# A three-layer graph network on one core: table scales from a bound, and the first layer's tables made while records are being scattered

## The chip, the core and the metric

The kernel runs on one core of a Trainium2 chip. The core has five engines with instruction streams of their own: TensorE (PE, matrix products; PEld is its weight load), VectorE (DVE), ScalarE (ACT), GpSimd (POOL) and SyncE (SP, which here only issues DMAs). They wait for one another on semaphores. SBUF holds the tiles, PSUM the results of PE. The metric is the device time of one execution in microseconds (us).

## The reference, cut to what matters

```python
N, E, D, EF, L = (3125, 100000, 128, 16, 3)      # nodes, edges, width, edge features, layers
s2 = jnp.concatenate([src, dst])                  # each edge in both directions
d2 = jnp.concatenate([dst, src])
ef2 = jnp.concatenate([ef, ef], axis=0)
h_prev = nf
for l in range(L):
    e_in = jnp.concatenate([h_prev[s2], h_prev[d2], ef2], axis=-1)
    msg = jax.nn.leaky_relu(e_in @ We1[l]) @ We2[l]
    red = jax.ops.segment_sum(msg, d2, num_segments=N)
    n_in = jnp.concatenate([h_prev, red], axis=-1)
    out = jax.nn.leaky_relu(n_in @ Wn1[l]) @ Wn2[l]
    h_prev = out + h_prev
x = _layernorm(x + out, axis=-1)                  # out of the last layer, before its addition to h_prev
```

## The kernel before

The nodes are padded to 3200, 25 blocks of 128, and lie transposed in SBUF (`hT`, 128 features by 3200 nodes). The part of `We1` that meets node features is applied once for each node and not for each edge. It gives two **tables** for each layer, `a = h @ We1[0:128]` and `b = h @ We1[128:256]`. Each table value is stored as a pair of 16-bit floats, a high half and a low half, scaled by a power of two so that they fit; plane 0 of a block is the high half, plane 1 the low one, and plane 2 holds plane 0 once more. Messages are then made by one-hot matrix products that pick table rows. Since `We2` is linear, it is moved behind the sum and multiplied into the node weights: `w21 = We2 @ Wn1[128:256]`.

The kernel runs through these stages on all engines:

- **Sorting**, up to 123 us: each edge gets a place in an order by pairs of node blocks. DVE is the busiest engine.
- **Scatters**, 123 to 1124 us: GpSimd issues 784 indirect DMAs (L651), each of which writes 128 edge records to `records` in DRAM. While they run, DVE and PE work out the places of the next records; they finish at 1082 us with the `map` and `word` tables (L1033 to L1035), which tell the loop which node block each tile of edges meets. At the end GpSimd waits until records have moved, reads two counts (L434, `live_counts`, in which `live_n` is the number of turns a layer needs, 26 here) and starts the next stage.
- **Preparation loop**, 1127 to 1198 us: 30 batches of records are loaded (`recc`), transposed by PE (L1283), copied by ACT and DVE to `recT` and `numT`, and written by SP to `feat_d` (two DMAs, L544) and `nums_d` (one, L547). When it ends SP appends a copy of the first pieces behind the last ones (L551, L552, "the wrap") and waits for that. Then it loads the first numbers (`load_numbers`, L556, two) and features (`load_features`, L563, six DMAs for three parts). `recT` lies in the tiles `numb` and `gsel`, which these loads and the one-hot of them (`gather_one_hot`, L1069) fill, so they could not start before the preparation loop is done.
- **Tables of the layer** (`tables(l)` on PE, L1299; L1079 to L1126 on DVE; L757 to L772 on ACT). PE makes a and b in 13 steps of two node blocks; ACT copies each from PSUM to SBUF (L757); DVE takes the largest magnitude of each copy (L1083, 13 of them) and of all (L1086); GpSimd takes it over all partitions (L675); DVE works out the scale (L1090 to L1103) and the scaled edge weights `wst` (L1107 to L1115). ACT then writes the high halves (L772, 5 parts), DVE plane 2 (L1122) and the low halves (L1123), and at last plane 2 of the lows in one copy of 3200 (L1126). In between ACT zeroes all of the PSUM sums (L760) and copies the transposed `We2` and `w21` (L765, L767).
- **Loop of the layer**: 26 turns of 12 steps, each step three tiles of 128 edges in both directions. PE starts with `start(l)` (its first product is L1342), then gathers (L1342, L1349) and sums (L1410); ACT copies and splits (L782 to L791); DVE applies leaky_relu and the low halves (L1065, L1136), in layer 0 also the one-hots (L1069, L1153). PE reads where to add from a row of words: layer 0 with L1416, layers 1 and 2 with `keep_row` (L1494), three of them ahead of the loop.
- **Node stage** (`node(l)`): ACT copies the sums out (L797), PE makes `z` (L1424, L1425), ACT copies it to `zbuf` (L802), DVE applies leaky_relu (L1065), PE makes `out` (L1430), DVE adds it to `hT` (L1182), ACT copies it to `outT` (L808). The PSUM banks of out are free for the next tables only after L808.
- **End**: after layer 2 SP loads x once more (`xn`, L612, into the place of the tables), PE transposes `outT` back, DVE adds `xn` (L1189) and normalises, SP writes the result.

Each queue runs in program order. SP also loads the weights: 15 DMAs at the start (L481 to L490), those of the next layer at each layer's end, the node weights only after `o_ps`, that is after L1430. The `xn` load stands behind the last of these, though the last layer has no next one. One `Fori(0, L)` loop covers the layers on ACT, DVE, GpSimd and SP.

## Time and profile before

| what | us |
|---|---|
| median of 3 runs | 3657.73 (3657.26 to 3658.81) |
| the profiled execution, its own time | 3661.46 |
| its span, first to last instruction | 3659.8 |
| scatters end (last L651) | 1124.0 |
| preparation loop, GpSimd's wait to the end of the wrap | 1124.0 to 1201.5 |
| first product of the loop (L1342), layer 0, 1, 2 | 1229.5, 2083.7, 2868.5 |
| node stages begin | 2029, 2818, 3602 |
| busy: PE, DVE, ACT, POOL | 2425.6, 2752.6, 2095.1, 777.5 |
| packets of instruction queues in the whole span | 14 and 10 |

The span is 1.7 us shorter than the profiled execution's own time, and that one lies 3.7 us above the median. Busy shares are averages over the stages. In the scatters GpSimd alone sets the pace; in the loop of layer 0 DVE has hardly a gap, in those of layers 1 and 2 PE. Between the loops no engine is busy throughout: there the chain of waits tells what counts.

### The profile page before, as it was taken

What the parts mean: (1) busy time and instruction counts of PE and PEld (TensorE: products, weight loads), DVE (VectorE), ACT (ScalarE), POOL (GpSimd) and SP (SyncE); (2) the same over time, 40 slices, a digit from 0 to 9 for tenths busy, and PEclk for the clock granted to TensorE, in tenths of its full rate; (3) what the DMA queues carried; (4) which work ended last, traced back from release to release, by engine and by line L of the source; (5) the groups of instructions that cost most, each with busy time, mean ns of one, the idle gap of its engine ahead of it and who ended that gap; (6) DMA issues with size and microseconds to landing.
All of it is one profiled execution on the core that took longest, in us unless ns stands there. A gap on an engine that the chain in (4) does not pass through costs nothing.

```text
span 3659.8 us, 81006 instructions
## 1 busy us (share of the span) xinstructions
PE 2425.6 (66%) x26726; PEld 2098.7 (57%) x26727; DVE 2752.6 (75%) x3366; ACT 2095.1 (57%) x4171; POOL 777.5 (21%) x826
## 2 busy tenths in 40 slices
PE   5000000000004699999999799999999799999995
PEld 4000000000003578787888588888887688888884
DVE  8956556565643899999999677777777777777775
ACT  4000000000003678787878688888887788888884
POOL 0477777777774000000000000000000000000000
PEclk9555555555557899999999899999999999999998
DMA  8111111111106477777777355555554355555553
GB/s 252 45 45 45 32 44 32 45 37 40 29 7 173 151 249 254 250 254 253 254 253 253 112 189 189 191 192 190 194 188 154 123 190 190 193 189 191 192 190 113
DMA packets 228758, 563.94 MB, mean 154 GB/s; under 512 B 43800, under 2 KB 125662, under 8 KB 228606
## 3 DMA queue, kind: packets, MB, share of 16 engines
q1 hardware_dynamic: 201182, 548.26, 44.3%
q0 software_dynamic: 27552, 15.37, 2.3%
q8 instruction: 14, 0.23, 0.0%
q14 instruction: 10, 0.08, 0.0%
HBM read 413.57 MB, written 150.16 MB: 154 GB/s over the span
## 4 chain that ended last, share of the span: by engine, by line
PE 49%; DVE 11%; issue 5%; DMA 1%; ACT 1%; SPq 1%; POOL 0%; DVEq 0%; ACTq 0%; POOLq 0%
PE gath L1349 18%; PE sums L1410 13%; PE sums L1349 9%; PE gath L1342 4%; DVE loop_buf L1136 3%; DVE big L1065 3%; PE sums L1342 2%; DVE loop_buf L1153 2%; DVE gsel L1069 2%; PE sums L1299 1%; PE sums L1424 1%; SPq L544 0%; PE sums L1425 0%; DMA ssel_d<-loop_buf 0%; ACT big L787 0%
## 5 line engine op out<-in xcount | busy, mean ns | idle before, releaser
L1065 DVE SCALAR_TENSOR_TENSOR big<-big 128x768 f32<-128x768 f32 (+1 forms) x957 | 907.6, 949 | 391.5 <-ACT big L787 353.1
L1349 PE MATMUL gath<-table,gsel 128*128 x7488 | 1075.4, 273 | 0.0
L1136 DVE TENSOR_TENSOR loop_buf<-big,loop_buf 128x768 f16<-128x768 f32 x936 | 889.5, 950 | 0.0
L651 POOL DMA_INDIRECT records<-rec,rowi x784 | 751.8, 959 | 285.2 <-issue 247.9
L1410 PE MATMUL sums<-loop_buf 128*128 128x128 f16 x11232 | 780.6, 219 | 16.5 <-issue 13.6
L1349 PEld LDWEIGHTS gath<-table,gsel 128*128 128x128 f16 x7488 | 734.0, 98 | 85.0
L791 ACT ACTIVATE loop_buf<-big 128x768 f16<-128x768 f32 x936 | 781.9, 835 | 0.0
L787 ACT ACTIVATE big<-gath 128x512 f32<-128x512 f32 x936 | 560.0, 598 | 272.8 <-PE gath L1349 272.8
L1410 PEld LDWEIGHTS sums<-loop_buf 128*128 128x128 f16 x11232 | 649.5, 98 | 105.6 <-ACT sums L785 33.4
L1257 PE MATMUL sums<-table,fchunk 128*128 128x200 f16 x196 | 37.1, 366 | 877.7 <-DVE found L977 865.3
L1349 PE MATMUL sums<-table,gsel 128*128 x3744 | 563.8, 273 | 14.0 <-DVE gsel L1069 13.9
L1257 PEld LDWEIGHTS sums<-table,fchunk 128*128 128x128 f16 x196 | 24.8, 136 | 889.8 <-issue 887.5
L732 ACT ACTIVATE rec<-big,sc_ef 128x448 f16 x28 | 18.7, 668 | 881.8 <-DMA records<-rec,rowi 881.8
L1342 PE MATMUL gath<-wst,fchunk 128*128 128x256 f16 x1872 | 511.7, 273 | 0.2 <-DMA loop_buf<-ssel_d 0.2
L782 ACT ACTIVATE big<-sums 128x256 f32<-128x256 f32 x936 | 353.3, 377 | 101.5 <-PE sums L1349 101.4
L1349 PEld LDWEIGHTS sums<-table,gsel 128*128 128x128 f16 x3744 | 361.4, 98 | 60.5 <-DVE gsel L1069 28.6
L785 ACT ACTIVATE sums<-iota 128x256 f32<-128x256 f16 x936 | 363.1, 388 | 29.5
L675 POOL PARTITION_ALL_REDUCE mxa<-mx x3 | 1.1, 358 | 1667.6 <-DVE mx L1086 1667.6
L1342 PE MATMUL sums<-wst,fchunk 128*128 128x256 f16 x936 | 255.9, 273 | 80.1 <-issue 80.1
L998 DVE SCALAR_TENSOR_TENSOR rowi<-rowb,rowc 128x28 int32<-128x28 int32 x28 | 5.3, 188 | 327.1 <-DMA records<-rec,rowi 326.8
L1342 PEld LDWEIGHTS gath<-wst,fchunk 128*128 128x128 f16 x1872 | 183.3, 98 | 32.3 <-DMA loop_buf<-ssel_d 0.5
L1153 DVE TENSOR_TENSOR loop_buf<-numc,iota 128x768 f16<-128x768 f16 x312 | 171.6, 550 | 4.1 <-DMA ssel_d<-loop_buf 0.5
(181 smaller groups left out, 1651.0 us busy)
## 6 DMA issues: line engine op xcount, KB each, us to landing
gsel<-gsel_d SPq DMA_DIRECT2D x208, 576.0 KB, 3.8
loop_buf<-ssel_d SPq DMA_DIRECT2D x208, 576.0 KB, 5.1
numb<-nums_d SPq DMA_DIRECT2D x106, 576.0 KB, 4.7
gsel_d<-gsel SPq DMA_DIRECT2D x104, 576.0 KB, 5.6
ssel_d<-loop_buf SPq DMA_DIRECT2D x104, 576.0 KB, 6.5
fchunk<-feat_d SPq DMA_DIRECT2D x630, 80.0 KB, 4.6
loop_buf<-rows_d SPq DMA_DIRECT2D x28, 896.0 KB
records<-rec,rowi POOLq DMA_INDIRECT x784
```

What stands on the lines that cost most here:

```text
L651: pool.indirect_dma_start(out=records[:, :], out_offset=bass.IndirectOffsetOnAxis(ap=rowi[:, h, g:g + 1].bitcast(U32), axis=0), in_=rec[:, ...
L782: act.activation(msg[:, place, 0:2 * D], gath6, ACT.Copy).then_inc(x6_set, 1)
L785: act.activation(gath6, iota[:, 0:2 * D], ACT.Copy, scale=0.0).then_inc(gath6_free, 1)
L787: act.activation(msg[:, place, 2 * D:MSG], gath[:, :], ACT.Copy).then_inc(x_set, 1)
L791: act.activation(m_hi[:, (q - 1) % RING, :], msg[:, (q - 1) % RING, :], ACT.Copy)\
L1065: return dve.scalar_tensor_tensor(m, m, SLOPE, m, ALU.mult, ALU.max)
L1069: dve.tensor_scalar(gsel[:, h, :], numb[:, h, :], part[:, 0:1], None, ALU.is_equal).then_inc(gsel_set[h], DMA)
L1136: dve.tensor_tensor(m_lo[:, place, :], msg[:, place, :], m_hi[:, place, :], ALU.subtract)\
L1153: last = dve.tensor_tensor(ssel[:, t % SLOTS:t % SLOTS + STEP, :, :].rearrange("p t s (e w) -> p (t s) e w", w=2), numc[:, 2 * t:2 * (t + ...
L1342: pe.matmul(uv, fchunk[:, p % PARTS, pair * P:(pair + 1) * P], wst[:, side, :, :].rearrange("p s f -> p (s f)"), start=fresh, stop=False, ...
L1349: return pe.matmul(uv, gsel[:, h, (2 * tc + s) * P:(2 * tc + s + 1) * P], at[n], start=False, stop=n == 3, skip_group_check=True)
L1410: last = pe.matmul(sum_at[i, s], m[:, place, w0:w0 + D], ssel[:, ts, s, :], start=False, stop=False, skip_group_check=True)
```

## The change

The change touches five places.

1. **The scale is bounded, not measured.** Once for all layers PE and DVE work out norms of the weights (of each matrix the largest sum of magnitudes over a column, by a product of ones with |w|). A bound on the largest magnitude of h, `h_bnd`, is kept: at first the measured one, then plus the bound on out, which is the largest magnitude of leaky z times the norm of `Wn2`. For that DVE reduces each bank of z (L1208 in the new file, 7 for a layer and one over them, L1212), GpSimd takes it over the partitions, and DVE works out the scale after the third of seven additions to `hT` (`SCALE_AT` is 3). The scale is thus known before the tables are made.
2. **The tables are made straight from PSUM.** ACT writes the high half of each of 13 steps from the PSUM bank, DVE the low half from the same bank in two instructions (L1112), and plane 2 of both halves in one copy (L1099). The copies L757, the 13 reductions L1083, L1122, L1123 and L1126 are gone. The zeroing of the sums (L760 on ACT) becomes `clear(l)` on PE, seven products of zeros (L1321), each after the low half of the bank it clears. The three `keep_row` loads (L1558 in the new file) stand behind it.
3. **Layer 0's tables and all of `w21` are made during the last scatters**: after `words_ready` (the end of L1035) SP, DVE, PE and ACT need not wait for GpSimd, and they do this work, with the memsets that stood at the end of the preparation loop, before they enter that loop. The 15 weight DMAs (of all layers at once) stand behind the last load of the scatters, none at the start or between layers.
4. **`recT` lies in the tile `big`** and no longer in `numb` and `gsel`, so the first `load_numbers` and `load_features` are issued inside the preparation loop, after its first half turn (`sp.If(it < 1)`). The wrap remains, but nothing waits for it before layer 0 starts. GpSimd reads `live_counts` before its wait for the records.
5. **Smaller ones.** `outT` is written in the last layer alone, straight from PSUM, and that layer has no addition to `hT`; the other layers don't wait for L808. GpSimd copies the node weights of the layer to `node_w`. DVE, ACT and GpSimd have the code of the layers three times instead of one loop over them.

The diff, cut (lines that only rename or move are left out; of `tables`, `scales` and `clear` the core stands here):

```diff
+        rec_words = PAIR_COLS * P // 2
+        recT = [big[0:2 * RW, NODES + k * rec_words:NODES + (k + 1) * rec_words].bitcast(F16) for k in range(SLOTS_IN)]
...
+            sp.wait_ge(rec_set, GROUPS + AHEAD)
+            sp.sem_inc(sp_go, 1)
+            sp.dma_start(we2, We2.rearrange("l k f -> k l f")).then_inc(w_in, DMA)
...
+            sp.dma_start(wn1a[:, :, :], Wn1[:, 0:P, :].rearrange("l k f -> k l f")).then_inc(w_in, DMA)
...
+                with sp.If(it < 1):
+                    sp.wait_ge(rec_out[0], 2 * 16 * OUT_DMAS)
+                    sp.sem_inc(sp_go, 1)
+                    for h in range(2):
+                        load_numbers(h, h)
+                    for p in range(F_AHEAD):
+                        load_features(0, p)
...
-                load_edge_weights((l + 1) % L)
-                sp.wait_ge(o_ps, (l + 1) * BANKS + AHEAD)
-                load_node_weights((l + 1) % L)
...
+            pool.wait_ge(map_in, 16)
+            live_n, live_p = live_counts(mybir.EngineType.Pool)
             for h in range(2):
                 pool.wait_ge(moved[h], 16 * GROUP * GTURNS + 16)
-            pool.wait_ge(map_in, 16)
-            live_n, live_p = live_counts(mybir.EngineType.Pool)
...
+            def node_weights(l):
+                pool.wait_ge(tables_set, (l + 1) * AB_STEPS)
+                pool.wait_ge(o_ps, l * BANKS + AHEAD)
+                pool.wait_ge(w21_set, 1)
+                pool.tensor_copy(node_w[:, 0, :], wn1a[:, l, :]).then_inc(node_w_set, 1)
...
+            for l in range(1, L):
+                pool.wait_ge(mx_set, l)
                 pool.partition_all_reduce(mxa[:, :], mx[:, :], P, bass.bass_isa.ReduceOp.max).then_inc(mx_all, 1)
+                node_weights(l)
...
+            def tables(l):
+                act.wait_ge(scw_set, l + 1)
+                act.wait_ge(halves_zero, 1)
+                wc = wts[:, l, 3, :]
+                act.activation(wch[:, :], wc, ACT.Copy, scale=sc_w[:, 0:1]).then_inc(wst_hi_set, 1)
...
+                for s in range(AB_STEPS):
+                    act.wait_ge(ab_ps, l * AB_STEPS + s + 1)
...
-                act.wait_ge(ab_set, (l + 1) * AB_STEPS)
-                act.activation(sums[:, :].rearrange("p (k w) -> p k w", w=2 * D),
-                               iota[:, 0:2 * D].unsqueeze(1).to_broadcast([P, BANKS * BANK // (2 * D), 2 * D]), ACT.Copy,
-                               scale=0.0).then_inc(sums_zero, 1)
...
-                    w = WIDE[n][1]
-                    act.wait_ge(o_ps, l * BANKS + n + 1 + AHEAD)
-                    act.wait_ge(h_set, l * BANKS + n + 1 + AHEAD)
-                    act.activation(outT[:, n * BANK:n * BANK + w], sums[:, n * BANK:n * BANK + w], ACT.Copy)\
-                       .then_inc(o_set, 1)
+            for n in range(BANKS):
+                w = WIDE[n][1]
+                act.wait_ge(o_ps, (L - 1) * BANKS + n + 1 + AHEAD)
+                act.activation(outT[:, n * BANK:n * BANK + w], sums[:, n * BANK:n * BANK + w], ACT.Copy)\
+                   .then_inc(o_set, 1)
...
+            dve.tensor_reduce(mx[:, :], hT[:, :], AX_X, ALU.max, apply_absolute_value=True).then_inc(h_max_set, 1)
+            dve.wait_ge(w_in, W_DMAS * DMA)
+            w_all = wts[:, :, :, :].rearrange("p l w f -> p (l w f)")
+            dve.scalar_tensor_tensor(w_abs, w_all, -1.0, w_all, ALU.mult, ALU.max).then_inc(abs_set, 1)
+            dve.wait_ge(h_max_set, 1)
+            dve.tensor_scalar(diag, ident[:, :], mx[:, 0:1], None, ALU.mult).then_inc(diag_set, 1)
+            dve.wait_ge(norms_ps, 1)
+            dve.tensor_reduce(norms[:, :, :].rearrange("p l w -> p (l w)"),
+                              sums[:, 2 * BANK:(2 + L) * BANK].rearrange("p (w f) -> p w f", f=D), AX_X, ALU.max)
...
+            def scales(l):
+                seq = l * 4
+                dve.scalar_tensor_tensor(bnd[:, :], h_bnd[:, :], ab_norm[:, l:l + 1], ef_bnd[:, l:l + 1], ALU.mult, ALU.add)\
+                   .then_inc(sc_seq, 1)
+                dve.wait_ge(sc_seq, seq + 1)
+                dve.tensor_scalar(ebits[:, 0:1], bnd[:, :].bitcast(I32), EXP_MASK, None, ALU.bitwise_and).then_inc(sc_seq, 1)
+                dve.wait_ge(sc_seq, seq + 2)
+                exponent(sc[:, 0:1], ebits[:, 0:1], 268, -1).then_inc(sc_seq, 1)
+                dve.wait_ge(sc_seq, seq + 3)
+                dve.tensor_scalar(sc_w[:, :], sc[:, 0:1], sc_ef[:, 1:2], 2.0 ** 120, ALU.mult, ALU.min).then_inc(scw_set, 1)
+                exponent(sc[:, 1:2], ebits[:, 0:1], -14, 1).then_inc(sc_seq, 1)
+                dve.wait_ge(sc_seq, seq + 4)
...
+            def plane2(l, s):
+                dve.wait_ge(tlo_set, l * AB_STEPS + s + 1)
+                dve.tensor_copy(halves_of[:, 2, ab_blocks(s), :, :], halves_of[:, 0, ab_blocks(s), :, :]).then_inc(tables_set, 1)
...
+                for s in range(AB_STEPS):
+                    dve.wait_ge(thi_set, l * AB_STEPS + s + 1)
+                    for k in range(2):
+                        last = dve.scalar_tensor_tensor(ab_table(s, 1)[:, k], ab_bank(s)[:, k], sc[:, 0:1], ab_table(s, 0)[:, k],
+                                                        ALU.mult, ALU.subtract)
+                    last.then_inc(tlo_set, 1)
+                    if s > 0:
+                        plane2(l, s - 1)
+                plane2(l, AB_STEPS - 1)
+            scales(0)
...
-                    dve.tensor_reduce(abmax[:, s, :], ab3[:, :, n0:n1], AX_X, ALU.max,
-                                      apply_absolute_value=True).then_inc(ab_maxed, 1)
...
-                    if b0 < NB:
-                        dve.tensor_copy(t_hi[:, 2, b0:min(b1, NB), :], t_hi[:, 0, b0:min(b1, NB), :])
-                    dve.scalar_tensor_tensor(two_planes[:, b0:b1, 1, :], ab_blocks[:, b0:b1, :], sc[:, 0:1],
-                                             two_planes[:, b0:b1, 0, :], ALU.mult, ALU.subtract).then_inc(tables_set, 1)
-                dve.wait_ge(tables_set, l * (T_PARTS + 1) + T_PARTS)
-                dve.tensor_copy(t_lo[:, 2, :, :], t_lo[:, 0, :, :]).then_inc(tables_set, 1)
...
+                    if l < L - 1:
+                        dve.wait_ge(zl_set, l * BANKS + n + 1)
+                        dve.tensor_reduce(zmax[:, n:n + 1], zbuf[:, n * BANK:n * BANK + w], AX_X, ALU.max,
+                                          apply_absolute_value=True).then_inc(zmax_set, 1)
+                if l < L - 1:
+                    dve.wait_ge(zmax_set, (l + 1) * BANKS)
+                    dve.tensor_reduce(mx[:, :], zmax[:, :], AX_X, ALU.max).then_inc(mx_set, 1)
+                    for n in range(BANKS):
+                        w = WIDE[n][1]
+                        part_n = slice(n * BANK, n * BANK + w)
+                        if n == SCALE_AT:
+                            dve.wait_ge(mx_all, l + 1)
+                            dve.scalar_tensor_tensor(h_bnd[:, :], mxa[:, :], norms[:, l, 2:3], h_bnd[:, :], ALU.mult, ALU.add)\
+                               .then_inc(h_bnd_set, 1)
+                            dve.wait_ge(h_bnd_set, l + 1)
...
+            def tables(l, after):
+                for s in range(AB_STEPS):
+                    if after is not None and s < BANKS:
+                        pe.wait_ge(h_set, after * BANKS + s + 1 + AHEAD)
+                    if s >= BANKS:
+                        pe.wait_ge(tlo_set, l * AB_STEPS + s + 1 - BANKS)
+                    for b in range(NB)[ab_blocks(s)]:
+                        last = pe.matmul(ab_bank(s)[:, :, b % 2, :], hT[:, b * P:(b + 1) * P],
+                                         wts[:, l, 0:2, :] if after is None else
+                                         wts[:, ds(l, 1), 0:2, :].rearrange("p a s f -> p (a s) f"), start=True, stop=True)
+                    last.then_inc(ab_ps, 1)
...
+            def clear(l):
+                for n in (BANKS - 1, *range(BANKS - 1)):
+                    s = n + AB_STEPS // BANKS * BANKS
+                    pe.wait_ge(tlo_set, l * AB_STEPS + (s if s < AB_STEPS else s - BANKS) + 1)
+                    pe.matmul(bank(n), zeros16[:, 0:P], zeros16[:, 0:BANK], start=True, stop=True, skip_group_check=True)
...
+            pe.wait_ge(abs_set, 1)
+            pe.wait_ge(diag_set, 1)
+            for l in range(L):
+                pe.matmul(bank(2 + l), ones[:, :], w_abs[:, l * WPARTS * D:(l + 1) * WPARTS * D], start=True, stop=True)
+            pe.matmul(bank(2 + L)[:, 0:P], ones[:, :], diag, start=True, stop=True).then_inc(norms_ps, 1)
+            pe.wait_ge(scw_set, 1)
+            tables(0, None)
...
-                tables(l)
+                tables(l, l - 1)
+                clear(l)
```

The `w21` products of all layers are made on PE and ACT ahead of the norms, in the same place.

On SP, at the end of the preparation loop, before:

```order
L547 DMA nums_d<-numT 64x128
L536 UNCONDITIONAL_BRANCH
L534 REGISTER_ALU
L534 COMPARE_AND_BRANCH
L549 ISA
L549 ISA [waits rec_out1,rec_out0]
L551 ISA [waits rec_out3,rec_out2]
L551 DMA feat_d<-feat_d 64x1920
L552 ISA
L552 DMA nums_d<-nums_d 16x288
L556 DMA numb<-nums_d 128x2304 [waits wrap_out]
L556 DMA numb<-nums_d 128x2304
```

and after, where the row L576 COMPARE_AND_BRANCH tests for the first turn:

```order
L575 DMA nums_d<-numT 64x128
L564 UNCONDITIONAL_BRANCH
L576 COMPARE_AND_BRANCH
L550 DMA numb<-nums_d 128x2304 [waits rec_out0]
L550 DMA numb<-nums_d 128x2304
L557 DMA fchunk<-feat_d 64x640 x6
L576 UNCONDITIONAL_BRANCH
L562 REGISTER_ALU
L562 COMPARE_AND_BRANCH
L585 ISA
L585 ISA [waits rec_out1,rec_out0]
L587 DMA feat_d<-feat_d 64x1920
```

The eight loads moved from behind the loop and behind the wrap into the loop; the wrap's DMAs are the last that SP issues before layer 0.

On DVE, from the end of the node stage (z has been through leaky_relu, L1065 before, L1144 after) to the first tables of the next layer. Before, one code for all layers, the jump L1076 leading from the end of a layer back to its start:

```order
L1065 SCALAR_TENSOR_TENSOR big<-big 128x128 [waits z_set]
L1182 TENSOR_TENSOR hT<-hT,sums 128x512 [waits o_ps] x6
L1181 REGISTER_ALU
L1182 TENSOR_TENSOR hT<-hT,sums 128x128 [waits o_ps]
L1076 REGISTER_ALU
L1076 COMPARE_AND_BRANCH
```

after, in the code of the first layer:

```order
L1212 TENSOR_REDUCE mx<-zmax 128x1 [waits zmax_set]
L1223 TENSOR_TENSOR hT<-hT,sums 128x512 [waits o_ps] x3
L1218 SCALAR_TENSOR_TENSOR h_bnd<-mxa,norms,h_bnd 128x1 [waits mx_all]
L1085 SCALAR_TENSOR_TENSOR bnd<-h_bnd,ab_norm,ef_bnd 128x1 [waits h_bnd_set]
...
L1223 TENSOR_TENSOR hT<-hT,sums 128x512 [waits o_ps] x2
L1223 TENSOR_TENSOR hT<-hT,sums 128x128 [waits o_ps]
L1107 SCALAR_TENSOR_TENSOR wst<-wts,sc_w,wch 32x256 [waits wst_hi_set]
L1107 SCALAR_TENSOR_TENSOR wst<-wts,sc_w,wch 32x256
L1112 SCALAR_TENSOR_TENSOR table<-sums,sc,table 128x2x128 [waits thi_set]
L1112 SCALAR_TENSOR_TENSOR table<-sums,sc,table 128x2x128
L1112 SCALAR_TENSOR_TENSOR table<-sums,sc,table 128x2x128 [waits thi_set]
```

The scale moved in between the additions to `hT`, and the low halves follow the last addition with only `wst` between them.

## Rows read from the trace of the kernel before

**Rows 1.** Windows: stretch, length, busy us of PE, PEld, DVE, ACT, POOL; clock, DMA, GB/s.

```profile
1083.00:1124.00 41.00, 0.00 (x0) 0.00 (x0) 0.00 (x0) 0.00 (x0) 29.65 (x31) 0.50 0.06 7
...
1198.00:1229.00 31.00, 7.81 (x37) 6.41 (x35) 21.58 (x40) 15.53 (x18) 0.36 (x1) 0.68 0.23 68
...
2056.00:2084.00 28.00, 11.72 (x54) 9.79 (x54) 20.96 (x36) 17.33 (x21) 0.35 (x1) 0.74 0.13 49
...
2841.00:2868.00 27.00, 11.22 (x51) 9.38 (x49) 20.97 (x36) 17.33 (x21) 0.36 (x1) 0.75 0.14 50
```

**Rows 2.** Chain of work that ended last, start, us, what: scatters' end, layer 0's start.

```profile
1125.28 0.72 POOLq L434
...
1227.81 1.73 issue
```

**Rows 3.** Timeline of SP: start, us, instruction; preparation loop to layer 0.

```profile
1194.92 0.82 SPq L544 DMA_DIRECT2D feat_d<-numb  x2
...
1201.54 0.86 SPq L556 DMA_DIRECT2D numb<-nums_d  x2
1202.44 5.62 SPq L563 DMA_DIRECT2D fchunk<-feat_d  x8
...
1247.91 2.60 SPq L563 DMA_DIRECT2D fchunk<-feat_d  x2
```

**Rows 4.** Timeline, tables of layer 0: start, us, instructions [idle before <-released by].

```profile
1192.57 12.60 PE L1299 MATMUL sums<-wab,hT 128*128 128x256 f32 x50 [1.58 <-DVE numb L1055]
...
1206.82 7.53 DVE L1083 TENSOR_REDUCE abmax<-big 128x2 f32<-128x512 f32 x13
...
1229.53 0.39 PE L1342 MATMUL sums<-wst,fchunk 128*128 128x256 f16 x1 [19.91 <-issue]
```

**Rows 5.** Source L1416, the read of words: duration min/median/max ns, first and last start.

```profile
L1416 PEldq TENSOR_LOAD <-word_row x27: 1102/1106/1316, 1210.3 to 2026.0; - x27
```

**Rows 6.** Timeline, DVE's and POOL's last work beside the scatters, and DVE's next.

```profile
1079.98 0.17 DVE L1033 TENSOR_TENSOR map_t<-map_t 128x3 int32<-128x3 int32 x1 [0.54 <-issue]
...
1090.21 0.96 POOL L651 DMA_INDIRECT records<-rec,rowi  x1 [2.50 <-issue]
1091.48 0.96 POOL L651 DMA_INDIRECT records<-rec,rowi  x1 [0.30 <-issue]
...
1130.68 0.45 DVE L1046 COPY num<-recc 128x64 f16<-128x64 f16 x1 [48.44 <-DMA recc<-records]
```

**Rows 7.** Windows, columns as in rows 1: scatters with DVE at work.

```profile
1019.00:1034.90 15.90, 0.00 (x0) 0.00 (x0) 15.61 (x10) 0.00 (x0) 11.97 (x13) 0.50 0.05 7
```

**Rows 8.** Timeline, additions to hT after layer 0, then the tables of layer 1.

```profile
2049.68 1.41 DVE L1182 TENSOR_TENSOR hT<-hT,sums 128x512 f32<-128x512 f32 x2
...
2053.84 0.89 DVE L1182 TENSOR_TENSOR hT<-hT,sums 128x512 f32<-128x512 f32 x2 [0.17 <-PE sums L1430]
...
2070.56 0.42 DVE L1115 TENSOR_TENSOR wst<-wcs,wch 32x256 f16<-32x256 f32 x1
...
2072.86 0.49 DVE L1122 COPY table<-table 128x1280 f16<-128x1280 f16 x1 [1.21 <-ACT table L772]
2073.27 1.55 DVE L1123 SCALAR_TENSOR_TENSOR table<-big,sc,table 128x1280 f16<-128x1280 f32 x1
...
2083.74 0.39 PE L1342 MATMUL sums<-wst,fchunk 128*128 128x256 f16 x1 [12.47 <-issue]
```

**Rows 9.** Source L1494, keep_row: duration min/median/max ns, first and last start.

```profile
L1494 PEldq TENSOR_LOAD <-map_row x84: 845/850/872, 2071.8 to 3599.4; - x84
```

**Rows 10.** Timeline, the end: last copy of outT and the additions of xn.

```profile
3623.18 0.77 ACT L808 ACTIVATE big<-sums 128x512 f32<-128x512 f32 x2 [0.26 <-DVE hT L1182]
...
3632.50 3.88 DVE L1189 TENSOR_TENSOR big<-sums,table 128x512 f32<-128x512 f32 x7 [9.21 <-DMA table<-x]
```

**Rows 11.** Chain of work, the same place.

```profile
3624.12 8.28 DMA table<-x
```

**Rows 12.** The page's queues: packets, MB, share of 16 engines.

```profile
q8 instruction: 14, 0.23, 0.0%
```

319 lines of the change are left out of this document (144 added, 175 removed).

## Prediction

> **What bounds the kernel now.** I read the table of busy shares first, and it is no guide here: DVE is busy for 75% of the span and PE for 66%, but each in stages of its own, and the change leaves the loops of the layers, nearly 2300 us, with the same instructions. What it touches are the seams between stages. So I read the windows over the seams. In the last 41 us of scatters PE, DVE and ACT do nothing, and only GpSimd works [rows 1]. In the 31 us ahead of the first loop and in the 28 and 27 us ahead of the other two, PE is busy for 8 to 12 us, DVE for 21, ACT for 16 to 17: no engine is full, a chain goes around them [rows 1]. The chain of waits names its links at layer 0: GpSimd's read of counts [rows 2], then SP's issues through the preparation loop, to its last batch at 1194.92, the wrap, the loads of numbers from 1201.54 [rows 3], the one-hot, DVE's reductions from 1206.82 [rows 4], the tables, and 1.73 us of issue [rows 2] until the first product at 1229.53 [rows 4]. Ahead of layer 1 it goes over the additions to hT, the copies and reductions, the scale and the two passes over the tables, up to 2083.74 [rows 8]. At the end it stands in a DMA of 8.28 us, x loaded again [rows 11], for which DVE sits idle 9.21 us [rows 10].
>
> **Part 1, the start of layer 0.** After the change the tables aren't on this path, if they are done before the preparation loop needs the engines. Room for them: DVE's last work for the scatters begins at 1079.98 and the `map` and `word` steps end at 1082.2; its next one begins at 1130.68 after 48.44 us of idleness [rows 6]. Need: five memsets and a reduction over 3200 columns (at 7.53 us for 6400 columns, [rows 4], 3.8 us), |w| over 1536 columns (1.9 at the rate of L1123, 1.55 for 1280, [rows 8]), the norms on PE (3.25 banks; I take 5.5 us from the slow clock of 0.50, [rows 1]), their reduction (1.8), the scale and `wst` (1.8), with the memsets about 20 us, so that the tables start near 1102. They take 13 steps of 1.0 to 1.3 us and end at 1116 to 1119, at least 11 us early. I count them as hidden.
>
> What is left on the path. GpSimd's read of the counts, 0.72 us [rows 2], now comes before its wait: minus 0.7. SP sets the pace of the preparation loop, so what is put into it counts: two loads of numbers at 0.86 for the pair and six of features. The eight of rows 3 took 5.62, 0.70 each, so 4.2; in layer 0's first part a pair took 2.60, 1.30 each, so up to 7.8. With the test of `it < 1` in seven more turns, for which no row stands (I take 0 to 1.5 us), the sum is 5 to 10; that SP waits in the first turns for the first batches anyway may hide a little. I take 8. PE was free for its tables at 1192.57 [rows 4]; it is now free at 1192.57 - 0.7 + 8 = 1199.9. Then `clear(0)`: seven products of zeros of 512 columns in 16 bits, about 0.33 each, 2.3 us; the read of words, 1.1 [rows 5]; and the start, 1.73 as before [rows 2]. First product at 1205.0 in place of 1229.53: **24.5 us gained**. Bounds: 5 us more in SP's part and a clear at twice the price give 17; the low ends give 27. The wrap's DMAs stay, but nothing in the first turns waits for them.
>
> **Part 2, before layers 1 and 2.** Before layer 1 the additions to hT begin at 2049.68 [rows 8]. Each reduction of z (0.58 for 512 columns, [rows 4]) lies behind a leaky_relu while PE makes the next bank; only that of the last bank and the one over all seven stand ahead of the additions: plus 1.5, a start at 2051.2. The seven additions end 5.05 us after their start (2053.84 + 0.89 - 2049.68, [rows 8]); they waited for PE at their end by 0.17 only, so I take them as unchanged, with 0.6 more for the scale's six small instructions among them: 2056.8. Two instructions for `wst` at 0.42 [rows 8]: 2057.7. Then 13 steps on DVE. L1123 takes 1.55 for 1280 columns and an addition 0.70 for 512 [rows 8]: 1.11 ns a column and 0.13 apiece, for 256 columns 0.35 to 0.42. The copy of 512 columns costs 0.24 to 0.28 (0.49 for 1280, [rows 8]). A step is 2 x 0.37 + 0.24 = 0.98, up to 1.12; 13 steps (the last is half) end at 2070.5, the last low half at 2070.2. ACT's part of a step, 0.6 us for 512 columns, and PE's two products keep ahead of that. Behind the last low half stand the last clear, 0.3; three `keep_row` loads at 0.85 to 0.92 with their issue, 2.75 [rows 9], which before ran beside the tables and now stand in front of the start; and the start, 1.2. First product at 2074.5, say 2074.7 in place of 2083.74: 9.0 gained. Steps of 1.12 give 7.2, and if PE issues the three loads faster or the additions hide the scale, 12. Before layer 2 the same engines are busy for the same times to 0.5 us [rows 1], so I count the same: **18.0 together**.
>
> **Part 3, the end.** SP issues the load of x as soon as the loop of layer 2 is done, near 3603, since it no longer stands behind the weights of a layer that does not exist. Its 8.28 us [rows 11] end some 12 us before they are needed. What is next is then the transposing of `outT`: its last copy ends at 3623.18 + 0.77 = 3623.95 [rows 10], now about 0.9 earlier without the additions to hT between, and the first result of PE comes 0.6 after it. The additions of xn start at 3623.7 in place of 3632.50 [rows 10]: **8.7 gained** (8 to 9.5).
>
> **At no cost**: the weight DMAs leave the first 123 us, but there DVE's sorting sets the time; behind the last load of the scatters they have 27 us and 6% of DMA time in use [rows 1]. GpSimd's three copies for the node weights lie in a stage in which it has nothing else to do. In the loops DVE loses the tests for the layer; nothing waited for them.
>
> **The sum**: 24.5 + 18.0 + 8.7 = 51.2. Against the profiled execution, 3661.46 - 51.2 = 3610.3; its own time is 3.7 above the median of the runs, and I carry the gain over to the median unchanged: 3657.73 - 51.2 = **3606.5**.
>
> **Rivals.** *A, the scatters grow longer.* DVE now works beside the last 31 scatters, and GpSimd sets the pace there. With DVE at work for 15.61 of 15.9 us, 13 scatters took 15.9 us, 1.22 each [rows 7]; with DVE idle 31 took 41.0, 1.25 each without the one gap of 2.50 [rows 1, 6]. That speaks against it. But those ten DVE instructions weren't 16-bit copies within SBUF. If each of the 14 plane copies (0.28), |w| (1.9), and the memsets and `diag` held GpSimd up for its own length, the scatters would be 7 us longer: 3613.5. The Trainium skill ("SBUF — State Buffer", section "Who interferes with whom") says that copies and tensor_scalar in a two-port mode lock GpSimd out for the whole instruction, and that DVE with two SBUF inputs contends with GpSimd's reads alone. By that rule this rival would come about.
>
> *B, the tables are late.* Small instructions of DVE ran at 0.70 us each before 1082, with 0.54 of it issue [rows 6]. If that held for the 60 instructions of the tables (42 us) behind 13 us of long ones, they would end near 1137, 6.5 us after 1130.68, and the start would be late by that: 3613.
>
> *C, slower: the loops fetch their code.* The loops' code on DVE, ACT and GpSimd now stands three times. One gap in GpSimd's scatters is 2.50 us of issue where the others are 0.30 [rows 6], 2.2 more, which may be the arrival of new code. If an engine's jump at the end of a turn cost 2.2 us in each of the 52 turns of layers 1 and 2, the time would be 3606.5 + 114 = 3721; from 24 turns on (51.2 / 2.2) the gain is gone. Against it: one queue of instructions carried 14 packets in the whole span [rows 12] and the other 10, though those loops turned 78 times; and a layer's loop on DVE gets shorter, not longer. The Trainium skill ("Runtime: NRT & Kernel Launch", section "Instruction fetch mechanics") holds a taken branch to a place outside two resident pages to be such a fetch. That 24 packets served all turns agrees with loops that lie within the pages.
>
> *D, the change doesn't give what it says.* If the preparation loop costs 12 us more and not 8, and each transition brings 7 because the additions to hT now wait for the scale, the gain is 20.5 + 14 + 8.7 = 43: 3614.5.
>
> **Chances.** Main case 0.66, A 0.13, B 0.08, D 0.10, C 0.03. A, B and D lie between 3613 and 3615, the two of them that may come together at 3620. The low end is all gains at their upper bounds, 27 + 24 + 9.5 = 60.5, 3597. Range 3596 to 3620. A measurement of this kernel tells about 0.2% (7.3 us) from no change. To fall within that, the change would have to lose 44 us of its gain; I know only C for a loss of that size, and leave a little for what I overlook: faster 0.95, same 0.02, slower 0.03.
>
> **What the profile of the changed kernel would show.** Part 1: DVE and PE busy between 1082 and 1119 and idle up to 1130; the pace of the scatters still 1.25 (A if it is more); SP with a stretch of some 6 us of loads after the second pair of batches; first product at 1205. Part 2: DVE full from the first addition to the last plane copy, in steps of 0.98; between the last low half and the first product 4.3 us of PE's loads and issue; 2074.7 - 24.5 = 2050 as the start of layer 1's loop. Part 3: DVE's wait ahead of L1189's successor released by PE and not by a DMA. The prediction is wrong if the layer loops change their length (about 800 us in layer 0 and 734 in layers 1 and 2), if DVE's tables end after 1130, or if one of the seams keeps a wait that I have not seen.

## The result: 62.7 us faster, 0.7 us below the range

The changed kernel took 3595.35 us, the median of four runs (3593.19 to 3597.54), against 3658.04 us of the kernel before (four runs, 3657.26 to 3658.81). The ratio is 0.9829, with a 95% interval of 0.9812 to 0.9846. The gain is 62.7 us where 51.2 was forecast, and the time lies 0.65 us below the range, which began at 3596. The profiled execution has a span of 3593.5 us and took 3595.21 us, so it lies on the median. That of the kernel before lay 3.4 us above its own. Some executions take about 85 us longer at a lower granted clock (two of the four of b_pad24, one of b_xn_early, two of the kernel before beside them), and no time or median given here counts them.

The seams come first, as in [rows 1]: windows of the changed kernel over the end of the scatters, the preparation loop, and the seams to layers 1 and 2 (stretch, length, busy us of PE, PEld, DVE, ACT and POOL, granted clock of TensorE, DMA share, GB/s).

```profile
1082.20:1130.40 48.20, 23.13 (x87) 17.02 (x87) 21.81 (x61) 11.66 (x20) 32.49 (x35) 0.64 0.12 29
1130.40:1199.60 69.20, 47.34 (x491) 36.66 (x490) 36.98 (x146) 30.19 (x57) 19.89 (x29) 0.80 0.87 246
1999.20:2035.80 36.60, 29.53 (x99) 17.60 (x99) 27.07 (x69) 17.29 (x30) 1.11 (x4) 0.96 0.23 80
2771.20:2809.50 38.30, 31.74 (x100) 18.24 (x101) 27.25 (x69) 17.26 (x30) 1.11 (x4) 0.88 0.06 23
```

PE, DVE and ACT, idle beside the last scatters in [rows 1], now work there for 23, 22 and 12 us. The third window holds the node stage of layer 0 with the seam behind it, and PE is busy in 29.5 of its 36.6 us.

DVE's timeline shows how early the tables of layer 0 are made (start, us, instructions, and in brackets the idle time before them with what ended it):

```profile
1079.84 3.49 DVE L1068 TENSOR_REDUCE mx<-hT 128x1 f32<-128x3200 f32 x1
...
1097.37 0.88 DVE L1112 SCALAR_TENSOR_TENSOR table<-sums,sc,table 128x256 f16<-128x256 f32 x2 [0.43 <-ACT table L775]
...
1111.49 0.42 DVE L1099 COPY table<-table 128x512 f16<-128x512 f16 x2
1126.75 0.19 DVE L1131 COPY num<-recc 128x64 f16<-128x64 f16 x1 [14.84 <-DMA recc<-records]
```

The last plane copy ends at 1111.91, and then DVE waits 14.84 us for the first records: there is that much room. In SP's timeline the loads of the first turns stand inside the preparation loop, and in PE's the start of layer 0 follows its last transposes:

```profile
1138.16 1.04 SPq L550 DMA_DIRECT2D numb<-nums_d  x2
1139.24 5.45 SPq L557 DMA_DIRECT2D fchunk<-feat_d  x6
```

```profile
1194.60 0.41 PE L1365 MATMUL gath<-ident,recc 128*68 128x128 f16 x4
1196.44 3.15 PE L1321 MATMUL sums<-zeros 128*128 128x512 f16 x7 [1.43 <-DVE big L1140]
1199.58 0.34 PE L1402 MATMUL sums<-wst,fchunk 128*128 128x256 f16 x1
```

Layer 0 begins at 1199.58 in place of 1229.53 [rows 4]. Ahead of layer 1, DVE's timeline (where [rows 8] shows that of before) and PE's first product behind it:

```profile
2013.27 1.87 DVE L1223 TENSOR_TENSOR hT<-hT,sums 128x512 f32<-128x512 f32 x3
2015.06 0.21 DVE L1218 SCALAR_TENSOR_TENSOR h_bnd<-mxa,norms,h_bnd 128x1 f32<-128x1 f32 x1
...
2016.25 2.08 DVE L1223 TENSOR_TENSOR hT<-hT,sums 128x512 f32<-128x512 f32 x4
2018.36 0.99 DVE L1107 SCALAR_TENSOR_TENSOR wst<-wts,sc_w,wch 32x256 f16<-32x256 f32 x2
...
2022.15 0.87 DVE L1112 SCALAR_TENSOR_TENSOR table<-sums,sc,table 128x256 f16<-128x256 f32 x2
```

```profile
2035.84 0.39 PE L1402 MATMUL sums<-wst,fchunk 128*128 128x256 f16 x1 [3.76 <-issue]
```

From the first addition to hT to the first product of layer 1 it is 22.57 us, 34.06 before. At the end, x is asked for at 3542.68 and DVE's additions wait for PE and no longer for a DMA [rows 10]:

```profile
3542.68 0.83 SPq L628 DMA_DIRECT2D table<-x  x1
...
3566.32 3.88 DVE L1230 TENSOR_TENSOR big<-sums,table 128x512 f32<-128x512 f32 x7 [5.59 <-PE sums L1601]
```

**Where the time went.** I cut each trace at instructions that both kernels have. "First records" is the time at which the DMA of the first records begins. A loop goes from its first product to ACT's first copy of the sums, a node stage from there to DVE's first addition to hT, a seam from there to the next loop's first product. "Before" is what three traces showed (the kernel before, and b_weights_late and b_pad2 below, which don't touch these stretches but for the stop spoken of there), "changed" what three executions of the changed kernel showed (it, a_again, a_again2). A fourth trace with the same code up to the end of layer 2, b_xn_early, is not in the means: it took 16.6 us for the node stage of layer 0, and with it the gain of that line would be 3.6 and not 4.4. In us; the gain is the difference of the means.

| stretch | before | changed | gain | forecast |
|---|---|---|---|---|
| scatters' end to the first records | 3.22 | 2.47 | 0.75 | 0.7 |
| first records to layer 0's first product | 101.9 to 102.3 | 76.1 to 77.2 | 25.6 | 23.8 |
| node stage of layer 0 | 19.5 to 20.6 | 14.1 to 16.8 | 4.4 | -1.5 |
| seam to layer 1 | 34.1 | 22.6 to 22.7 | 11.4 | 10.5 |
| node stage of layer 1 | 14.3 to 15.5 | 14.0 to 15.7 | -0.4 | -1.5 |
| seam to layer 2 | 33.8 to 34.1 | 22.6 | 11.3 | 10.5 |
| node stage of layer 2 to the additions of xn | 27.1 to 28.7 | 18.5 to 21.3 | 7.4 | 8.7 |
| three loops | 2272.2 to 2273.9 | 2270.2 to 2270.5 | 2.5 | 0 |

The gains make 63.0. The stretches left out, up to the scatters' end and behind the first addition of xn, were 1.2 and 0.1 us shorter, so that these traces differ by 64.1 us where the medians of the runs differ by 62.7. The loops' 2.5 us belong to no edit that I can name, and may be chance in part: the five other kernels below with the changed loops took 2271.2 to 2272.9. The surprise is the third line.

### The profile page after: what moved, and what is told of

The parts are those of the page before. It is cut to its first block, busy times and chain, and to the rows that moved or that the text cites. A ratio compares the mean times of both kernels' runs of the same rounds, so it can differ in the third digit from the quotient of the medians.

```text
span 3593.5 us, 80512 instructions
## 1 busy us (share of the span) xinstructions
PE 2437.8 (68%) x26755; PEld 2105.2 (59%) x26756; DVE 2745.6 (76%) x3411; ACT 2063.7 (57%) x4144; POOL 779.1 (22%) x834
## 4 chain that ended last, share of the span: by engine, by line
PE 49%; POOL 21%; DVE 14%; issue 13%; DMA 1%; SPq 1%; ACT 1%; DVEq 0%; POOLq 0%; ACTq 0%
POOL records L666 21%; PE gath L1409 18%; PE sums L1470 13%; PE sums L1409 9%; PE gath L1402 5%; DVE loop_buf L1164 3%; DVE big L1144 3%; PE sums L1402 2%; DVE loop_buf L1181 2%; DVE gsel L1148 2%; DVE table L1112 1%; DVE table L897 1%; PE sums L1486 1%; PE sums L1487 0%; PE sums L1365 0%
## 5 line engine op out<-in xcount | busy, mean ns | idle before, releaser
L1144 DVE SCALAR_TENSOR_TENSOR big<-big 128x768 f32<-128x768 f32 (+1 forms) x957 | 908.6, 950 | 382.7 <-ACT big L813 356.1
L1470 PE MATMUL sums<-loop_buf 128*128 128x128 f16 x11232 | 781.2, 219 | 17.0 <-issue 14.1
L757 ACT ACTIVATE rec<-big,sc_ef 128x448 f16 x28 | 18.7, 668 | 881.0 <-DMA records<-rec,rowi 881.0
L808 ACT ACTIVATE big<-sums 128x256 f32<-128x256 f32 x936 | 352.3, 376 | 102.5 <-PE sums L1409 102.3
```

The source lines that it names most:

```text
L808: act.activation(msg[:, place, 0:2 * D], gath6, ACT.Copy).then_inc(x6_set, 1)
L1144: return dve.scalar_tensor_tensor(m, m, SLOPE, m, ALU.mult, ALU.max)
L1470: last = pe.matmul(sum_at[i, s], m[:, place, w0:w0 + D], ssel[:, ts, s, :], start=False, stop=False, skip_group_check=True)
```

## The experiments

I had two theories of the 11.5 us beyond the forecast. *Theory A*: the seams brought what was forecast, and the rest came from PE's code. In the kernel before, PE stops in layer 0's node stage to fetch code, and the change moved the place of that code, not the work. *Theory B*: the rest comes from what the change does, above all from the weight loads that left the first 123 us and from the node stage's own instructions. The rows of PE that raised it, in the kernel before (columns as above):

```profile
2031.69 1.56 PE L1425 MATMUL sums<-big,w 128*128 128x512 f32 x2
2036.51 2.08 PE L1424 MATMUL sums<-hT,wn 128*128 128x512 f32 x2 [3.26 <-issue]
```

PE stops for 3.26 us with nothing to wait for that the profile shows. The views of DMA queues over loop 0's first turns (1230 to 1290) and over the node stage (2030 to 2042) show instructions arriving: packets, MB, share.

```profile
q8 instruction: 4, 0.07, 0.4%
...
q8 instruction: 2, 0.03, 1.0%
```

In the same windows of the changed kernel (1200 to 1260, 1999 to 2011) it is five packets and one, and PE runs through:

```profile
q8 instruction: 5, 0.08, 0.5%
...
q8 instruction: 1, 0.02, 0.5%
```

```profile
2000.95 1.02 PE L1487 MATMUL sums<-big,node_w 128*128 128x512 f32 x2
2001.81 1.02 PE L1486 MATMUL sums<-hT,node_w 128*128 128x512 f32 x2
```

Each packet brings 16,384 bytes. The Trainium skill ("Runtime: NRT & Kernel Launch", section "Instruction fetch mechanics") says that code comes in pages of 16 KiB, 256 instructions, that a jump outside of the resident ones is a fetch, and that crossing a boundary is mostly hidden. The packet's size agrees; the stop does not: it isn't hidden.

### b_pad24: the kernel before with PE's code moved

Ahead of the first product of zeros, long before loop 0, PE makes 24 more products of zeros (48 instructions), at a place where it has time.

```
+            for _ in range(24):
+                pe.matmul(gath[:, 0:CHAINS * NB], zeros16[:, 0:P], zeros16[:, 0:CHAINS * NB], start=True, stop=True,
+                          skip_group_check=True)
             pe.matmul(gath[:, 0:CHAINS * NB], zeros16[:, 0:P], zeros16[:, 0:CHAINS * NB], start=True, stop=False,
```

> The kernel before with 24 small products of zeros more, early in PE's program where PE waits for DVE anyway; nothing else differs. Theory (code page): the 3.26 us of issue that PE spent in the middle of the first node stage of the kernel before, and the products at half clock behind it, come from PE waiting for its next page of code, because a page ended there by chance. Moving PE's code by 24 products takes the page's end out of that place: from the first copy of the sums to the first addition to hT 14.0 to 15 us in place of 19.70, and the median 3 to 5.5 us lower, about 3653 to 3655. Rival (the weights' DMAs or the stage itself make PE wait there): 19.7 stays, the median stays at 3658.

It took 3653.66 and 3655.29 us, against 3657.23, the median of the kernel before in the same comparison: 1.9 to 3.6 us faster for 24 products more. Two executions settle little, since those of the kernel before lie between 3654.6 and 3661.0; the trace says more. The node stage took 14.48 us, and the row of the stop is gone:

```profile
2031.15 1.73 PE L1428 MATMUL sums<-big,w 128*128 128x512 f32 x2
2032.67 1.91 PE L1427 MATMUL sums<-hT,wn 128*128 128x512 f32 x2
```

The packets are now five in loop 0's first turns and one here, as in the changed kernel. Theory A holds for this stage of the kernel before: whether PE stops hangs on where its code lies. (A trace with before's code on PE, b_xn_early, has the stop too, but a shorter one of 1.86 us and a stage of 16.6: there it is worth 2 us.) The gain of the whole is smaller, since the padding starts the scatters 0.9 us later than in b_xn_early (at 123.39) and the stretch ahead of layer 0 took 1.6 us more (103.78).

The stop isn't the whole difference. Windows over four node stages, with TensorE's granted clock: the kernel before after layer 0, b_pad24 after layer 1, and, after layer 0, the changed kernel and a_again (the changed kernel run once more).

```profile
2029.98:2049.68 19.70, 15.70 (x31) 6.69 (x32) 4.27 (x7) 7.48 (x14) 0.00 (x0) 0.74 0.28 94
2813.85:2826.63 12.78, 12.04 (x31) 5.68 (x32) 4.27 (x7) 7.48 (x14) 0.00 (x0) 1.00 0.03 9
1999.19:2013.27 14.08, 13.25 (x34) 6.25 (x35) 8.64 (x15) 7.47 (x14) 0.00 (x0) 1.00 0.58 206
1999.40:2016.19 16.79, 15.96 (x34) 7.30 (x35) 8.83 (x15) 7.58 (x14) 0.00 (x0) 0.81 0.47 167
```

At the full clock (1.00, 2.4 GHz) the stage takes 12.78 us with the code of before and 14.08 with that of the changed kernel, so the change makes it 1.3 us longer. The 19.70 us are these 12.78, the stop of 3.26, and 3.7 us that PE's products lose while the clock is at 0.50 (1.2 GHz), which it was from 2032.0 to 2042.3. b_pad24's stage of layer 0 lost 1.7 us in that way, and those of the changed kernel 0 to 2.7. So of the 5.2 us between 19.70 and 14.48, 3.3 are the stop and 2.0 the clock. The low clock isn't simply the stop's doing: in the kernel before it began 1.2 us ahead of the stop, and a_again has it for 6.8 us without one. It lasted 10.2 us in four of the five traces with a stop, 3.4 in the fifth (b_xn_early), and 0 to 6.8 without. What sets its length isn't shown.

### b_pad2 and b_pad128: how the stop moves

The same edit with 2 products (4 instructions) and with 128 (256 instructions, one packet's worth).

> The kernel before with 2 small products of zeros more, early on PE, so that all later code lies 4 instructions further. In the kernel before PE stopped in the first node stage behind 8 instructions (4 passes of weights and products), for 3.3 us of issue, and went on 1.4 us after a page of code had landed. Theory (the resident code ends at a fixed place of PE's program): PE stops 4 instructions earlier, so behind the first two passes of L1424's pair and ahead of L1425's, and the stage takes 16.5 to 20 us. Rival (what stops PE is tied to the stage's own work, not to the place of the code): it stops behind L1425's pair again.

> The kernel before with 128 small products of zeros more, early on PE, so that all later code lies 256 instructions further, one page of 16 KB in which it is fetched. Theory A (only the place within a page counts): the stop behind 8 instructions of the first node stage is back, as in the kernel before, 16.5 to 20 us for the stage. Theory B (the resident code reached 8 pages from the program's start in the kernel before, and one page more is fetched in the first turn of the loop where the code lies further on): no stop, 12.8 to 16.8 us, as with 24 products more. The changed kernel with 102 products more speaks for B.

Single executions: 3659.99 and 3661.94 us. PE's rows of b_pad2, and then of b_pad128:

```profile
2028.23 1.13 PE L1427 MATMUL sums<-hT,wn 128*128 128x512 f32 x2 [2.76 <-ACT big L797]
2034.02 2.08 PE L1428 MATMUL sums<-big,w 128*128 128x512 f32 x2 [4.67 <-issue]
```

```profile
2034.62 1.65 PE L1428 MATMUL sums<-big,w 128*128 128x512 f32 x2
2039.19 2.08 PE L1427 MATMUL sums<-hT,wn 128*128 128x512 f32 x2 [2.92 <-issue]
```

In the kernel before PE ran two products of hT and two of big (eight instructions) and then stopped. Four instructions of padding make it stop after the two of hT, four instructions earlier. A full page of padding puts the stop back where it was, which is what Theory A of that expectation said. So it is a boundary in PE's program that comes back after 256 instructions, and nothing in the work. What PE waits for can be seen too: in all five traces with a stop a packet of q8 is under way during it, and PE goes on 1.4 to 1.5 us after the packet has landed (in the kernel before it was under way from 2034.1 to 2035.1, and PE went on at 2036.51). Theory A holds for the kernel before. B fell for this stage, since at the same clock the change's own instructions lengthen it by 1.3 us.

### b_weights_late: the weights out of the first 123 us

The twelve weight loads of layer 0 move behind the last loads of the scatters; nothing else changes.

```
-            load_edge_weights(0)
-            load_node_weights(0)
...
+            load_edge_weights(0)
+            load_node_weights(0)
             sp.wait_ge(map_ready, 1)
```

> The kernel before with the 12 weight DMAs of layer 0 issued behind the last loads of the scatters, not at the start. Theory (the transfers compete with the first inputs): DVE's first instruction comes 1.7 us earlier (8.85 in place of 10.54) and the first scatter at 122.7 in place of 124.36; the time falls by 1.7, 3656.3. The prediction's view (DVE sets the time of the first 123 us, weights cost nothing): no change, first scatter at 124.4.

3657.67 against 3657.23 us, ratio 1.0002 (0.9993 to 1.0012): nothing. Its trace starts DVE at 8.93 and has 998.28 us of scatters, where the profiled kernel before shows 10.54 and 999.67. But b_xn_early, with the weights still at the start, has 8.68 and 997.94. Those 3 us were of that one execution, and are its 3.4 above the median. This part of Theory B fell.

### b_xn_early: the end alone

The kernel before, without the loads of a layer 3 ahead of the load of x.

```
-                load_edge_weights((l + 1) % L)
-                sp.wait_ge(o_ps, (l + 1) * BANKS + AHEAD)
-                load_node_weights((l + 1) % L)
+                with sp.If(l < L - 1):
+                    load_edge_weights((l + 1) % L)
+                    sp.wait_ge(o_ps, (l + 1) * BANKS + AHEAD)
+                    load_node_weights((l + 1) % L)
```

> The kernel before, where the weight loads at a layer's end are left out for the last layer, so that the load of x is issued as soon as the loop of layer 2 is done. Prediction's view: DVE's additions of x start 7.4 to 8 us earlier (28.7 us after the first copy of the sums before, 20.9 to 21.3 now), time 3650 to 3650.6. Rival (the load of x shares DMA engines or is late for another reason): less than 4 us.

3650.13 us, 7.1 less than the kernel before (ratio 0.9979, 0.9969 to 0.9989). The additions of xn now wait for PE, as in the changed kernel:

```profile
3618.39 3.88 DVE L1190 TENSOR_TENSOR big<-sums,table 128x512 f32<-128x512 f32 x7 [1.41 <-PE sums L1538]
```

### a_tables_late: the tables of layer 0 put back

The changed kernel with the making of layer 0's tables behind the preparation loop again, on PE, ACT and DVE. The diff moves these calls, with the norms and products ahead of them.

```
-            scales(0)
-            tables(0)
             dve.wait_ge(map_in, 16)
...
+            scales(0)
+            tables(0)
             dve.wait_ge(numb_in[0], 16)
```

> The changed kernel, with the products w21, the norms, the scale and the tables of layer 0 made behind the preparation loop and not during the last scatters. Theory: this work lies wholly under the scatters in the changed kernel, and took 32 us there, of which the tables 14.6. Now it is on the path: first product of layer 0's loop 27 to 32 us later, near 1229, time 3623 to 3627. Rival (something else, the first loads by SP, would hold the start anyway): under 15 us.

3627.41 us, 32 more than the changed kernel; the first product of layer 0 comes at 1230.50, 31 us later. PE's last product of the preparation ends at 1195.12, so it is 35.4 us from there to the start, 38.5 in the kernel before and 4.6 in the changed one. In its timeline the 50 products for the tables wait for the scale, which waits for a reduction that begins when the preparation is over:

```profile
1196.45 3.49 DVE L1134 TENSOR_REDUCE mx<-hT 128x1 f32<-128x3200 f32 x1 [0.74 <-issue]
...
1211.43 12.72 PE L1311 MATMUL sums<-wts,hT 128*128 128x256 f32 x50 [3.59 <-DVE sc_w L1078]
```

All but 4.6 us is hidden in the changed kernel, at no cost that a trace shows. The whole gain of 25.6 is owed to where this work stands. With it put back, the way from the first records to layer 0 is 107.4 us, 5 more than in the kernel before: the loads cost the preparation loop more, and what the bound and the tables from PSUM bring, 3 us behind it with the norms paid for, does not make up for that.

### a_again and a_loads_late: what the loads cost the preparation loop

a_again is the changed kernel once more, to compare with. a_loads_late takes the first turns' loads out of the preparation loop and puts them behind it, as they stood before.

```
-                with sp.If(it < 1):
-                    sp.wait_ge(rec_out[0], 2 * 16 * OUT_DMAS)
...
             sp.wait_ge(wrap_out, 32)
+            for h in range(2):
+                load_numbers(h, h)
+            for p in range(F_AHEAD):
+                load_features(0, p)
```

> The changed kernel once more, unchanged, as the measure for the three beside it and to see which segments of its trace repeat. Expected: 3595.3, first scatter near 122.5, scatters 998.0 to 998.4 long, from the first copy of the sums to the first addition to hT 14.1 after layer 0 and 12.8 to 15.7 after layer 1. The 19.5 us of the kernel before should not show up.

> The changed kernel, with the first loads of numbers and features issued behind the preparation loop and the wrap, as in the kernel before, and not after its first half turn. Prediction's view: the loads cost 7.5 to 8 us in the loop, since SP sets its pace, so PE is free 8 us earlier (1187); but then wrap, loads, their landing and the one-hot follow one another, and the first product of layer 0's loop comes 4 to 6 us later than 1199.6: time 3599.5 to 3601.5. Rival (the loads hide in the loop, since SP waits for the first batches anyway): PE free at the same time, first product 11 us or more later, 3606 or more.

3593.61 and 3600.97 us. PE's rows of a_loads_late:

```profile
1189.01 2.64 PE L1317 MATMUL sums<-zeros 128*128 128x512 f16 x7 [1.43 <-DVE big L1136]
...
1206.01 0.39 PE L1398 MATMUL sums<-wst,fchunk 128*128 128x256 f16 x1 [14.35 <-DMA fchunk<-feat_d]
```

Counted from the first records, PE begins the clear after 64.8 us in place of the 73.3 of a_again, but the first product then waits 14.35 us for features and comes 5.4 us later (81.8 against 76.4). So the loads cost the loop 8.5 us where the forecast had 8, and are still worth having in it.

### a_copies: does work on DVE hold up GpSimd's scatters?

Rival A by itself: 20 copies of 576 columns in 16 bits within SBUF, and a fill, beside the scatters of the changed kernel.

```
+            for place in spare:
+                dve.tensor_copy(place, zero_half)
             scales(0)
```

> The changed kernel with 20 copies more on DVE, 128 by 576 in 16 bits within SBUF, one behind the other just ahead of the scale of layer 0, so beside the scatters, and a fill of 128 by 2304 before them. Theory from the trace (the 14 copies of plane 2 lengthened two scatters by 0.24 us in all): the scatters take 998.3 to 999 us, no more. Rival (a copy holds GpSimd up for its whole length, the rule of the Trainium skill on the shared port): 20 x 0.3 = 6 us more, 1004, and the first product 6 us later. The tables end 7 to 9 us later than 1112, still before 1126.75, so that nothing else should move.

One execution: 3599.86 us; scatters 998.56 us, 998.46 in a_again. Eight copies of DVE and GpSimd's timeline beside them:

```profile
1094.75 1.95 DVE L1126 COPY numb<-gsel 128x576 f16<-128x576 f16 x8
```

```profile
1095.31 1.06 POOL L666 DMA_INDIRECT records<-rec,rowi  x1 [0.30 <-issue]
1096.68 1.07 POOL L666 DMA_INDIRECT records<-rec,rowi  x1 [0.30 <-issue]
1098.05 1.06 POOL L666 DMA_INDIRECT records<-rec,rowi  x1 [0.30 <-issue]
```

Three scatters took 0.10 us more each, 0.31 together for 4.7 us of copies, and the stretch as a whole isn't longer. Rival A fell: a scatter is held up for less than one copy, not for the sum of them. The start of layer 0 didn't move (76.63). The whole execution took 6.3 us more than the median of a_again, the very size that the rival named, but its trace has none of it in the scatters: against the trace of a_again, the loops took 2.5 us more, the node stage of layer 0 1.0 less, and those of layers 1 and 2 1.7 and 2.8 more. The Trainium skill ("SBUF — State Buffer", section "Who interferes with whom") holds copies in a two-port mode to lock GpSimd out for the whole instruction, and DVE with two SBUF inputs to contend with its reads. Of the first the runs show a tenth of a microsecond for each scatter. The second agrees with one row of the changed kernel: |w| reads two inputs for 1.75 us from 1083.24, and the scatter that began beside it took 1.52 us, while the one already under way took the usual 0.96. But it cost nothing: the next scatter began 2.68 us later, as at every turn of GpSimd's loop (0.96 and a gap of 1.72).

```profile
1083.04 0.96 POOL L666 DMA_INDIRECT records<-rec,rowi  x1 [0.30 <-issue]
1084.30 1.52 POOL L666 DMA_INDIRECT records<-rec,rowi  x1 [0.30 <-issue]
1086.98 0.95 POOL L666 DMA_INDIRECT records<-rec,rowi  x1 [1.17 <-issue]
```

### a_again2 and a_pad102: the stop back into the changed kernel

a_pad102 adds 102 products of zeros behind the tables of layer 0, which by PE's count of instructions should bring the page boundary back into the node stage.

```
+            for _ in range(102):
+                pe.matmul(gath[:, 0:64], zeros16[:, 0:P], zeros16[:, 0:64], start=True, stop=True, skip_group_check=True)
             pe.wait_ge(map_in, 16)
```

> The changed kernel unchanged, beside the one with 102 products more on the same chip: 3593.6 to 3595.4, the stage at 14.1 to 16.8 us.

> The changed kernel with 102 small products of zeros more on PE, behind the tables of layer 0, where PE waits for the scatters to end (their results are overwritten). They move PE's code behind them by 204 instructions, so that the first node stage starts at the same place of a 256-instruction page as in the kernel before (21 instructions into a page, in the count of the compiled program). Theory (a page of code that ends in the node stage): in the first turn of layer 0's loop four pages are fetched and not five, two are fetched in the node stage, PE spends 3 us of issue between its products there, and from the first copy of the sums to the first addition to hT it takes 18 to 20 us in place of 14.1 to 16.8; the time rises by 3 to 5 us. Rival (the change itself, without outT's wait or with GpSimd's node weights, shortened that stage): 14.1 to 16.8 stays, and the time is that of the changed kernel.

3594.09 and 3598.19 us. The packets came as forecast: four in loop 0's first turns and two in the node stage.

```profile
q8 instruction: 4, 0.07, 0.4%
...
q8 instruction: 2, 0.03, 1.1%
```

But PE didn't stop, and the stage took 16.84 us where 18 to 20 was expected:

```profile
2002.79 1.92 PE L1489 MATMUL sums<-big,node_w 128*128 128x512 f32 x2
2004.49 1.91 PE L1488 MATMUL sums<-hT,node_w 128*128 128x512 f32 x2
```

That expectation failed. The 16.84 us are those of a_again (16.79), with the same clock of 0.81 and no stop. The median rose by 4.1 us, within the 3 to 5 that the theory gave, but not for its reason: the stage took 1.1 us more than in a_again2, by the clock, and the two profiled executions, 0.3 us apart, don't show the rest. A page that comes at this time doesn't by itself stop PE. So why the changed kernel has no stop isn't shown: which page stops PE, and whether the code's offset in memory differs between the kernels, stays open.

### a_best: three more steps of the same kind

The changed kernel with three edits: PE's three keep_row reads go ahead of the tables; the writing of the numbers in the preparation loop goes to ACT, for one of each two batches; the output leaves in two parts, the first behind 14 blocks.

```
             with pe.Fori(1, L) as l:
...
+                for j in range(-LAG_LOADS, 1):
+                    keep_row(j, 0)
                 tables(l, l - 1)
                 clear(l)
                 pe.sem_inc(pe_go, 1)
...
-                for j in range(-LAG_LOADS, 1):
-                    keep_row(j, 0)
                 start(l)
```

```
+                        act.dma_start(nums_d[ds(first * (2 * BATCH), 2 * BATCH), :], numT[:, half * 2, :])\
...
+            sp.dma_start(out[0:14 * P, :].rearrange("(b p) f -> p b f", p=P), y[:, 0:14, :]).then_inc(s_out, 16)
+            sp.wait_ge(y_set, 2)
```

> The changed kernel with three edits. (1) The three reads of rows ahead of layers 1 and 2 are issued before the tables and not behind the clearing: if the 3.76 and 3.56 us of issue ahead of the first product are mostly these reads, the way from the first addition to hT to the first product falls from 22.6 to about 20.1, twice; if the issue is of the start itself, it stays. (2) In the preparation loop ACT issues one of the two nums_d DMAs of each pair of batches: if SP's issues set the pace, the loop is 0.5 to 0.75 us per pair shorter, 7.5 to 11 us in all; if another engine or the transfers are next at once, under 3 us. (3) The output's DMA is issued in two parts, the first after 14 of 25 blocks: 1.5 to 2.5 us from DVE's normalising to the end; none if the fixed part of a DMA decides. Sum by the theory: 14 to 18 us, 3577 to 3581.

3584.71 us (3584.24 to 3587.56), 8.9 less than a_again and 0.9805 of the kernel before (0.9789 to 0.9822): it beats both kernels. The first products of layers 1 and 2 stand behind 1.31 and 1.20 us of issue in place of 3.76 and 3.56:

```profile
2033.68 0.39 PE L1411 MATMUL sums<-wst,fchunk 128*128 128x256 f16 x1 [1.31 <-issue]
```

Each seam lost 2.6 us, and the end lost 2.8 (24.37 from the additions of xn). The stretch from the first records to layer 0 gave only 3.5 (72.9 against 76.4) where 7.5 to 11 was expected. With less for SP to issue, PE's transposes (21%) and the DMAs that write the features (20%) are the longest parts of its chain of waits from 1130 to 1165. One step of the latter is:

```profile
1145.19 7.15 DMA feat_d<-big
```

## Why the prediction missed, step by step

**The step that failed** is the node stage of layer 0 in Part 2: "only that of the last bank and the one over all seven stand ahead of the additions: plus 1.5, a start at 2051.2". It took this stage as it was before, 19.7 us, and added 1.5: 21.2 us. The changed kernel needed 14.1 to 16.8. Of the 11.5 us beyond the forecast this is the largest part, 5.9 in the means.

What was wrong is the 19.7 carried over, not the 1.5 added. Layer 0's node stage held a stop of PE (3.26 us of issue in the trace of before, 2.96 and 1.86 in b_weights_late and b_xn_early) and products at half the clock around it. The prediction never looked into this stage, since the change adds only reductions there. In the changed kernel there was no stop and less of the low clock, which gave 4.4 us of gain in place of 1.5 of loss. b_pad24 loses the stop without the change, and b_pad2 and b_pad128 show that the stop moves with the code's position: the kernel before could have had this part of the gain without what the change does. That the position alone freed the changed kernel of it isn't shown, since a_pad102 didn't bring it back.

The 1.5 itself was nearly right. Compared at the full clock, the stage is 1.3 us longer after layer 0 (14.08 against 12.78) and 1.2 after layer 1 (14.02 in a_again). In the changed kernel the last leaky_relu ends at 2012.84 and the additions begin at 2013.27, 0.43 us for the last reduction, of 128 columns, and the one over all seven; the rest is that this leaky_relu comes 0.8 us later, behind the reduction of the bank ahead of it (0.69). The table's 0.4 us of loss in layer 1's stage mixes executions at different clocks.

**The range failed with it.** Its low end was the sum of every listed gain at its upper bound. No term stood for what a stage may lose that the change only touches, so no bound reached the 4.4 us, nor the 2.5 us of the loops. Without these two the time would have been near 3602, inside the range.

**Part 1, the start of layer 0**: 24.5 forecast, 26.4 measured (0.75 for the counts' read, 25.6 behind it). The preparation loop lengthened as said: from the first records to PE's last product 63.7 us before, 71.5 now, so 7.8 for the forecast 8 (8.7 in the means of the three traces each). a_loads_late shows the same cost from the other side, 8.5. Two small terms were off. The 12.60 us of [rows 4] stand behind 1.58 us of idleness, so PE was done 1.6 us before 1192.57, and I counted from there. And the read of words and the start ran under the clear: it took 3.15 us (2.3 forecast), but the first product followed directly, where I had added 1.1 and 1.73. That the tables are wholly hidden was right, with 14.84 us to spare and the end at 1111.9, ahead of 1116 to 1119.

**Part 2, the seams themselves**: forecast 23.5 us from the first addition to the first product (2051.2 to 2074.7), measured 22.6. A step of the tables takes 0.985 us, as forecast; the additions with the scale's small instructions among them took 5.06 us from start to end, 5.6 forecast; and from the last low half to the first product it was 4.2, 4.3 forecast. This term was right to 4%.

**Part 3, the end**: 8.7 forecast, 7.4 in the mean. The releaser is PE as said. b_xn_early shows 7.1 for this edit alone. The rest is the node stage of layer 2, which took from 18.5 us (a_again) to 21.3 (the changed kernel), where PE's clock fell to 0.50 for 6.8 us.

**At no cost**, the weight loads: right, by b_weights_late.

**Rivals.** A fell to a_copies; the scatters took 998.3 us as in the kernels before. B fell: 14.84 us of room. D fell: the loop cost 7.8 to 8.7 and each seam gave 11.3 to 11.4. C fell: 15 and 13 packets of instructions in the page (q8 and q14), where [rows 12] has 14, and no longer loops.

```profile
q8 instruction: 15, 0.25, 0.0%
q14 instruction: 13, 0.11, 0.0%
```

But the reading under C was mostly wrong as well. Of the gap of 2.50 us in GpSimd's scatters [rows 6], 1.72 aren't new code: such a gap comes every 112 scatters (142.8 us) in all kernels, at a turn of its loop. This one had 0.8 on top, and one packet of q14, the other queue of instructions, arrived within it. Whether that is the cause isn't shown: b_xn_early has the plain 1.73 there, a_tables_late 2.17. C asked the right question, what fetching code costs, of the wrong engine: PE had paid it in layer 0's node stage.

## What to carry to other kernels

Before you sum the terms of a change, read every stage that its code passes through for waits that are "issue" alone, also those that it hardly touches: a stop that hangs on the code's position can come or go with an edit, and the range has to hold it. Compare a stage before and after only at the same granted clock: here that turned a seeming loss of 0.4 us into 1.2. A chain of small steps around several idle engines is worth more than a busy share suggests: 23 us of PE's work and 22 of DVE's cost nothing beside scatters that another engine makes. Where a queue of DMA issues sets a loop's pace, as SP's does here, count every issue that is put into it. Giving some of them to another engine brought less than their length here (3.5 us of the 7.5 to 11 expected), since PE's transposes and the transfers were next.

## What the runs showed of the hardware

- A stop of PE behind its long loop, during which a packet of 16,384 bytes of instructions arrived, cost 1.9 to 4.7 us, and ended 1.4 to 1.5 us after the packet had landed. In the kernel before it moved with the position of the code (4 instructions of padding put it 4 instructions earlier, 48 took it away, 256 put it back). Not each fetch at that place stops PE (a_pad102).
- In most node stages the granted clock fell from 1.00 (2.4 GHz) to 0.50 (1.2 GHz) for 3.4 to 10.2 us, with a stop or without. Pairs of products took 1.91 us there in place of 1.02.
- A scatter of GpSimd beside 16-bit copies of DVE took 1.06 in place of 0.96 us. One that began beside an instruction of DVE with two inputs of 1536 columns in SBUF took 1.52, and the gap behind it was shorter by as much.
- GpSimd's loop of scatters has a gap of 1.72 us in place of 0.30 every 112 scatters, in every kernel (the last of the six differs, 1.17 to 2.50).
- Reads of words by PE (0.85 to 1.1 us each) cost nothing while products are queued ahead of them, and their full length behind a wait: moving three of them ahead of the tables gave 2.6 us at each seam.
